# Moving two of the h products within each batch: chunk 2's to ahead of tile 6, the next batch's first to ahead of tile 13

## The reference

```python
Bx  = einsum('bni,bri->bnr', x, cond_B[id])          # 512 x 16 per entry
c   = einsum('bnr,bor->bno', Bx, cond_A[id])         # 512 x 2048
base   = c @ base_w.T + base_b
hidden = c @ ffn_A.T                                  # rank 64
probs  = softmax(c @ router_w.T)                      # 16 experts
combine = top-2 of probs, normed
out = x + base + 0.5 * sum_e combine[e] * (hidden @ expert_B[e].T)
```

## Time and profile before

| | |
|---|---|
| median of 3 executions | 440.36 us (439.89 to 441.36) |
| the profiled execution | 441.32 us, span 439.2 us |
| granted TensorE clock | 0.999 of full |
| busy: PE, DVE, ACT, POOL | 404.6, 325.5, 111.6, 40.2 us |
| busy PE, 180 to 220 us | 40.0 of 40 us |
| busy DVE, 180 to 220 us | 30.6 of 40 us |
| DMA | 135.35 MB, mean 308 GB/s |

### The profile page before, as it was taken

The page is one execution under the profiler, slowest core; times in us unless marked ns, Lnnn a source line. Parts: engine busy times, 40 slices in busy tenths (PEclk is TensorE's granted clock), DMA queues, the critical chain, the costliest instruction groups (busy, mean ns, idle before and its releaser), DMA issues.

```text
span 439.2 us, 6803 instructions
## 1 busy us (share of the span) xinstructions
PE 404.6 (92%) x2496; PEld 278.9 (64%) x2496; DVE 325.5 (74%) x838; ACT 111.6 (25%) x171; POOL 40.2 (9%) x53
## 2 busy tenths in 40 slices
PE   0487997989899999999999999999999999999996
PEld 0374985657566766656667667666666676666665
DVE  2699997999566697768849775976779497755453
ACT  0003213436284321233131222312231321224110
POOL 4010000001200021012010201200120111012000
PEclk9999999999999999999999999999999999999999
DMA  8999999999998999999999999999999999756835
GB/s 221 357 330 334 338 359 371 341 283 323 301 297 200 300 357 323 284 342 378 302 306 348 325 344 298 390 295 289 362 357 312 294 360 334 282 203 233 323 140 191
DMA packets 75027, 135.35 MB, mean 308 GB/s; under 512 B 5506, under 2 KB 14770, under 8 KB 74994
## 3 DMA queue, kind: packets, MB, share of 16 engines
q1 hardware_dynamic: 56000, 102.08, 71.8%
q10 hardware_dynamic: 18994, 32.84, 25.6%
HBM read 99.23 MB, written 35.65 MB: 307 GB/s over the span
## 4 chain that ended last, share of the span: by engine, by line
PE 71%; DVE 10%; DMA 9%; SPq 6%; ACTq 1%; issue 1%; ACT 1%; DVEq 0%
PE ps L945 15%; PE ps L919 13%; PE ps L946 13%; PE ps L947 13%; PE ps L948 6%; PE ps L961 6%; DMA bexpT<-in_x 6%; DVE early L684 4%; DVE xT L750 3%; DMA gm_r<-xT 3%; SPq L319 3%; PE ps L874 2%; PE ps L970 1%; PE ps L884 1%; SPq L262 1%
## 5 line engine op out<-in xcount | busy, mean ns | idle before, releaser
L860 DVE TENSOR_TENSOR xbuf<-ps,xbuf 128x512 f32<-128x512 f32 x128 | 86.1, 674 | 81.4 <-PE ps L948 81.3
L945 PE MATMUL ps<-h_r,u_r 128*128 128x512 f32 x256 | 105.4, 412 | 0.7 <-DVE xbuf L860 0.7
L946 PE MATMUL ps<-h_r,u_r 128*128 128x512 f32 x256 | 100.3, 392 | 0.0
L947 PE MATMUL ps<-h_r,u_r 128*128 128x512 f32 x256 | 99.9, 390 | 0.0
L884 PE MATMUL ps<-early 128*128 128x256 f32 x256 | 64.7, 399 | 25.4 <-DVE early L684 25.4
L750 DVE STREAM_TRANSPOSE xT<-xbuf 128x256 f32<-128x256 f32 x224 | 80.4, 410 | 0.0
L884 PEld LDWEIGHTS ps<-early 128*128 128x128 f32 x256 | 47.0, 196 | 39.2 <-issue 17.2
L684 DVE STREAM_TRANSPOSE early<-xbuf 128x256 f32<-128x256 f32 x128 | 66.2, 577 | 5.4 <-issue 4.0
L945 PEld LDWEIGHTS ps<-h_r,u_r 128*128 128x128 f32 x256 | 48.0, 188 | 34.6 <-issue 22.6
L919 PE MATMUL ps<-bexpT,cur 128*32 128x512 f32 x512 | 61.6, 598 | 1.5 <-DVE h_r L732 1.5
L518 ACT ACTIVATE h_r<-ps 128x512 fp32r<-128x512 f32 x64 | 36.3, 594 | 89.4 <-PE ps L919 86.5
(11 more groups left out here) (73 smaller groups left out, 213.5 us busy)
## 6 DMA issues: line engine op xcount, KB each, us to landing
out<-xbuf SPq DMA_DIRECT2D x31, 1024.0 KB, 9.9
xbuf<-in_x SPq DMA_DIRECT2D x28, 1024.0 KB, 9.1
xbuf<-in_x ACTq DMA_DIRECT2D x32, 512.0 KB, 10.4
xbuf<-in_x SPq DMA_DIRECT2D x32, 512.0 KB, 13.2
xbuf<-in_L_ffn_base_w SPq DMA_DIRECT2D x16, 512.0 KB, 19.0
xbuf<-in_L_ffn_base_w ACTq DMA_DIRECT2D x16, 512.0 KB, 19.3
gm_r<-g_hilo SPq DMA_DIRECT2D x128, 32.0 KB, 9.0
early_u<-in_L_ffn_B SPq DMA_DIRECT2D x10, 256.0 KB, 17.8
```

The lines of the kernel that those rows point to most:

```text
L860: dve.tensor_tensor(xs, ps[:, tile_bank(b.n, m), :], xs, ALU.add).then_inc(s_out, 1)
L945: pe.matmul(acc, u_r[:, b.q, 0, h, tok_t], hi, start=(h == 0), stop=False)
L946: pe.matmul(acc, u_r[:, b.q, 0, h, tok_t], lo, start=False, stop=False)
L947: pe.matmul(acc, u_r[:, b.q, 1, h, tok_t], hi, start=False, stop=False)
```

## The change

The fixed places of the h products (ahead of the first tile of each chunk) become a table. Batch 0 keeps its own: 0, 4, 8, 12. In batches 1 to 7 they are 0, 6, 8 and 13. So chunk 2's product goes from ahead of tile 4 to ahead of tile 6, where PE issues it directly before the second half of Bx; and the product for the next batch's chunk 0 goes from ahead of tile 12 to ahead of tile 13, behind the flips, which stand behind tile 12. `h_split_at` gives the places of the splits on ACT and DVE: a tile after the product (1, 9 and, new, 14), except for the product at 6, whose split is at 6 itself (before: 5).

```diff
--- before.py
+++ after.py
@@ -292,7 +292,21 @@
 
             return [p for p in wanted if p[0] < NB]
 
-        H_LO_AT = 1
+        H_FIRST = (0, NT, 2 * NT, 3 * NT)
+        H_LATER = (0, NT + 2, 2 * NT, 3 * NT + 1)
+
+        def h_ahead_of(b, f, m):
+
+            last = f is not None and f.n < 2
+            at = H_FIRST if b.n == 0 or last else H_LATER
+            if m not in at:
+                return None
+            c = at.index(m)
+            return (b, c + 1) if c + 1 < OC else (f, 0) if f is not None else None
+
+        def h_split_at(b, f, m):
+
+            return h_ahead_of(b, f, m - 1) if b.n == 0 or m < NT or m >= 2 * NT else h_ahead_of(b, f, m)
 
         Steps = namedtuple("Steps", "bxp bx_lo logits peak exp spread top comb comb_k flips u")
         FIRST_STEPS = Steps(8, 9, 9, 9, 9, 10, 10, 11, 12, 13, {13: (0,), 14: (1,)})
@@ -623,11 +637,8 @@
             def step(b, f):
                 for c in range(OC):
                     for t in range(NT):
-                        if t == H_LO_AT:
-                            if c < OC - 1:
-                                h_hi(b, c + 1)
-                            elif f is not None:
-                                h_hi(f, 0)
+                        if h_split_at(b, f, c * NT + t):
+                            h_hi(*h_split_at(b, f, c * NT + t))
                         if b.n == 0 and c * NT + t in E_LATE:
                             copy_experts(E_LATE[c * NT + t])
                         for n, g in present(refills(b.n, c * NT + t)):
@@ -846,11 +857,8 @@
                 for c in range(OC):
                     for t in range(NT):
                         m = c * NT + t
-                        if t == H_LO_AT:
-                            if c < OC - 1:
-                                h_lo(b, c + 1)
-                            elif f is not None:
-                                h_lo(f, 0)
+                        if h_split_at(b, f, m):
+                            h_lo(*h_split_at(b, f, m))
                         dve.wait_ge(s_acc, b.n * MT + m + 1)
                         if b.n == 0 and m % 2 == 0:
                             dve.wait_ge(s_xres[c // 2 * 2 + t // 2], 32)
@@ -1005,11 +1013,9 @@
                     h_products(first, 0)
             def step(b, f):
                 for c in range(OC):
-                    if c < OC - 1:
-                        h_products(b, c + 1)
-                    elif f is not None:
-                        h_products(f, 0)
                     for t in range(NT):
+                        if h_ahead_of(b, f, c * NT + t):
+                            h_products(*h_ahead_of(b, f, c * NT + t))
                         for n, span in present(bx_groups(b.n, c * NT + t)):
                             bx_products(Batch(n), span)
                         tile_products(b, c, t)
```

## The result

The changed kernel took 443.9 us (median of four, 443.71 to 444.93) against 440.28 us for the kernel before (median of four, one execution more than at the time of the prediction): ratio 1.0071, 95% interval 1.0045 to 1.0097. It is slower by 3.6 us, by the interval by 2.0 to 4.3 us; forecast were +2.8 us and 443.2.

A forecast was written before the change was run, and what follows sets the result against it. PE's in-order steps were taken to bound the kernel; +0.81 for the flips' wait and -0.35 for the merge gave +0.46 us a batch, in six batches +2.8, so 443.2 us, range 441.3 to 445.4.

The forecast's parts named there:

- The bound: PE, 92% busy, goes through its program in order from batch 1 on; time is the sum of its steps.
- Part one, -0.35: Chunk 2's h ahead of tile 6 shares one gap with Bx's second half: -0.35 us a batch in batches 1 to 6.
- the second rival: The flips wait but the switches save nothing: +4.9 us, 445.3; chance 0.10.
- Part two, the wait: Flips right after tile 12 wait about 1 us per batch for ACT's spread combine weights, in batches 1 to 6.
- Part two, +0.81: Tile 13's last matmul comes at 241.45 instead of 240.64: +0.81 us a batch, bounds +0.66 to +1.13.
- The saving without a wait, -0.15: Next batch's h behind the flips takes one PE switch less: 0.1 to 0.19 us a batch saved if the flips don't wait.
- The first rival: The merges gain and the flips do not wait: -0.35 - 0.15 each batch, -3.0 us, 437.4; chance 0.11.
- The late split of h(0): DVE's split behind tile 13's addition makes PE's next h wait for nothing, with 0.4 and 0.8 us to spare.
- The sum: +0.81 - 0.35 = +0.46 us a batch, in six batches +2.8 us.

The follow-up runs named there:

- the two parts alone: Against the kernel before: only chunk 2's h ahead of tile 6 (ratio 0.9985, repeated 0.9956); only the next batch's first h ahead of tile 13 (1.0137).
- the move alone: Kernel before with chunk 2's h ahead of tile 5, where no Bx stands, instead of tile 4: ratio 0.9994 to the kernel before.
- The run without the wait: Changed kernel with DVE's low-half split of chunk 3's h ahead of tile 8's addition instead of tile 9's: 438.3 us, ratio 0.9940 to the kernel before.
- The run with h first: Changed kernel with the next batch's h issued before the flips between tiles 12 and 13, split still at 14: ratio 0.9998 to the kernel before.

## Why the prediction was right, and which terms were off
- **The bound.** PE runs through its program, and a batch's period is the sum of its steps. Right: the two parts alone add up to the whole within 0.01 us a batch. Bx's second half starts 0.4 us earlier, though, not within 0.1 of its old place (behind tile 3's last matmul 5.23 us, before 5.61); nothing waited for that.
- **Part one, -0.35.** Right, -0.36 alone (39.52), and by the merge, since the move alone is worth 0.0. That also decides against the second rival. The prediction's account of the 0.35 was incomplete: 0.32 instead of 0.23 ahead of h and 1.51 instead of 1.36 behind it make 0.24. The rest is in the middle: from h's start to Bx's it is 219.16 - 217.42 = 1.74 us, from h's to a tile's 236.65 - 234.80 = 1.85. What PE does in these 0.35 us no run shows. The sentence in the Trainium skill, "TensorE: Matmul & The Clock Gate", "The mechanism", that loads overlap only when the row group differs does not hold for these tiles, but what contradicts it is the loads of 0.19 us hidden between matmuls 0.227 apart, and not the merge. The same section also allows a load into a background weight buffer, which the trace agrees with and the prediction left out.
- **Part two, the wait.** Right in place, cause and size: the flips wait for ACT's copies, at the end of a chain that is tied to tile 8's addition. Taking the split out of the chain, whose end then comes 1.2 us earlier, removes the loss; letting the flips start 0.52 us earlier gives back 0.43 of the 0.55; and h as a cover removes it too.
- **Part two, +0.81.** It was +0.91, inside the stated ends. In before's frame the flips started at 236.61 + 0.57 = 237.18, not 237.3: a released PE needed 0.06 us, the load and the matmul together. But from the flips to h it is 1.02 us instead of 0.79. The run without the wait has 236.25 - 235.29 = 0.96 there, so a switch from flips to h costs 0.17 more than one from flips to a tile, beyond the 0.09 that I had as an upper end. The two errors point opposite ways, -0.12 and +0.23, so that the sum is nearer than its terms; that is luck.
- **The saving without a wait, -0.15.** Mis-sized for the same reason, since the 0.17 eats most of the 0.19: 239.60 - 233.47 = 6.13 us from tile 11's to tile 13's last matmul against 6.16, so this merge is worth 0.03 us there, and 0.06 to 0.08 by the periods (39.46, and 39.44 with h first, against 39.52). The first rival's 437.4 would have been 6 x -0.42 = -2.5, 437.9.
- **The late split of h(0).** I gave it 0.4 us to spare at its first half. Both subtractions were done at 244.40, before the next h started, so it had 0.7 (the first one ended 0.6 earlier). The run with h first, where PE was ready for the next h 1.0 us sooner against ACT's copies and waited, shows how near that was.
- **The sum.** Predicted +0.46 a batch, measured +0.55; +2.8 us predicted, +3.3 from the periods, +3.6 from the medians.

## What to carry to other kernels
Where one engine is busy without a gap, price an edit on it by the distance between two fixed instructions; and then ask of every step that this engine now reaches sooner when its input was ready, not whether it ever waited: a wait of 0.0 in the profile can be a slack of 1.27 us, used up by moving its cover of 2.09. A step that is moved out of a full queue belongs where the queue stands idle, and its own consumers must be listed first: moved the other way, the same split made the kernel 11 us slower than the one before, some 3 of them by the clock.

## What the runs showed of the hardware that was not expected
- After 1.8 us of idle PE the granted clock fell to 0.50 in two batches of one kernel, about 1 us after PE had started again, and stayed at 1.00 in three others after the same idle time (windows above, two of the three not shown). The changed kernel's idle time of 0.7 us left it at 1.00.
- Steps of matmuls with 32 output rows cost 0.35 us less when they stand next to each other (h with Bx, as the earlier trace rows had it and the move confirmed). New was that the flips (128x128) next to h save next to nothing, 0.03 to 0.08 us: from flips to h it is 0.96 us, from flips to a tile 0.79.
